# When ScalarE evacuates the down products: behind tanh, ahead of the fp16 conversion and the down weights

## What is computed

```
x  = L0_attn_x                              # 4 x 256 x 512
xn = _layernorm(x)
# attention: q 32 heads, k and v 8 heads, width 16, causal
weights = softmax(where(causal, -inf, q @ k.T) * 16 ** -0.5)
attn    = (weights @ v) @ Wo + bo
# experts: sigmoid scores, top 4 of 16, weights normalised
g, u = xn @ Wg[e].T, xn @ Wu[e].T           # 512 -> 256
out += cw[:, e] * ((silu(g) * u) @ Wd[e].T) # 256 -> 512
out += (silu(xn @ Sg.T) * (xn @ Su.T)) @ Sd.T
x + attn + out
```

## Time and profile before

| what | value |
|---|---|
| median of 3 runs | 598.5 us (597.1 to 607.98) |
| profiled execution, its own time | 602.74 us |
| its span, first to last instruction | 601.0 us |
| mean granted TensorE clock | 0.929 |
| TensorE matmuls busy | 474.4 us (79%) |
| VectorE busy | 372.9 us (62%) |
| ScalarE busy | 260.0 us (43%), 385 instructions |
| GpSimd busy | 251.3 us (42%) |

### The profile page before, as it was taken

The page is one execution under the profiler, slowest core; times in us unless marked ns, Lnnn a source line. Parts: engine busy times, 40 slices in busy tenths (PEclk is TensorE's granted clock), DMA queues, the critical chain, the costliest instruction groups (busy, mean ns, idle before and its releaser), DMA issues.

```text
span 601.0 us, 10314 instructions
## 1 busy us (share of the span) xinstructions
PE 474.4 (79%) x2984; PEld 349.3 (58%) x2984; DVE 372.9 (62%) x656; ACT 260.0 (43%) x385; POOL 251.3 (42%) x224
## 2 busy tenths in 40 slices
PE   0993679689976987889859788898688889889970
PEld 0872557456754764567636464676456647667640
DVE  6189866766863685448838881668556715966420
ACT  0531111255544473445547642556555425645610
POOL 3000491046544552264436672354445534545420
PEclk9996889879998997979979989999989989989986
DMA  7713924166355457655396945555853463425322
GB/s 288 290 54 93 306 65 126 70 207 175 68 156 132 74 142 201 122 141 98 66 247 189 270 100 107 109 147 116 247 148 62 82 116 65 80 54 82 45 36 35
DMA packets 33502, 78.26 MB, mean 130 GB/s; under 512 B 4960, under 2 KB 12640, under 8 KB 30240
## 3 DMA queue, kind: packets, MB, share of 16 engines
q0 software_dynamic: 11936, 27.53, 25.3%
q1 hardware_dynamic: 14064, 41.60, 20.9%
q10 hardware_dynamic: 7440, 8.39, 6.1%
HBM read 54.04 MB, written 23.33 MB: 129 GB/s over the span
## 4 chain that ended last, share of the span: by engine, by line
PE 47%; DVE 18%; issue 11%; ACTq 8%; ACT 6%; DMA 5%; POOL 2%; DVEq 1%; SPq 0%; POOLq 0%
PE psum L1051 26%; PE psum L1178 5%; DMA k_pack<-k_parts 4%; DVE negm L871 3%; PE psum L1012 2%; PE psum L1188 2%; ACT wsplit L517 2%; PE psum L1075 2%; PE psum L1144 2%; PE psum L1160 2%; ACTq L627 2%; ACTq L253 1%; ACTq L539 1%; PE psum L1061 1%; DMA xn<-x 1%
## 5 line engine op out<-in xcount | busy, mean ns | idle before, releaser
L1051 PE MATMUL psum<-wsplit,xgT 128*128 (+1 forms) x660 | 178.3, 421 | 9.2 <-DVE xgT L756 9.2
L1051 PEld LDWEIGHTS psum<-wsplit,xgT 128*128 128x128 f32 x660 | 128.2, 201 | 37.7 <-issue 9.8
L422 POOL DMA_INDIRECT out<-ysb,tab x48 | 83.3, 1736 | 128.2 <-ACT ysb L550 118.7
L1051 PE MATMUL psum<-wsplit,zT 128*128 (+1 forms) x336 | 98.9, 433 | 19.6 <-DVE zT L863 19.6
L1051 PEld LDWEIGHTS psum<-wsplit,zT 128*128 128x128 f32 x336 | 64.9, 204 | 38.4 <-issue 25.5
L591 ACT ACTIVATE xn<-psum 128x1536 f32<-128x1536 f32 x32 | 46.4, 1451 | 53.0 <-PE psum L1146 33.8
L402 POOL DMA_INDIRECT xg<-xn_rows,tab x47 | 51.2, 1089 | 39.5 <-PE psum L1188 22.1
L871 DVE TENSOR_REDUCE negm<-psum 128x4 f32<-128x512 f32 x64 | 58.4, 950 | 9.4 <-PE psum L1080 9.3
L911 DVE TENSOR_TENSOR xgT<-psum,xgT 128x512 fp32r<-128x512 f32 x47 | 32.3, 688 | 51.0 <-ACT xgT L513 45.9
L504 ACT ACTIVATE th<-psum 128x256 f32<-128x256 f32 x55 | 21.2, 386 | 95.5 <-PE psum L1051 92.7
L427 POOL TENSOR_TENSOR wsplit<-wraw,wsplit (+1 forms) x16 | 39.6, 2476 | 51.4 <-ACT wsplit L517 47.2
(11 more groups left out here) (174 smaller groups left out, 642.1 us busy)
## 6 DMA issues: line engine op xcount, KB each, us to landing
wraw<-wexp SPq DMA_DIRECT2D x17, 1024.0 KB
wraw<-wexp SPq DMA_DIRECT2D x17, 512.0 KB
q_parts<-stage ACTq DMA_DIRECT2D x36, 64.0 KB
q_pack<-q_parts ACTq DMA_DIRECT2D x6, 384.0 KB, 5.7
xn<-x SPq DMA_DIRECT2D x4, 512.0 KB, 5.7
xn_rows<-xn SPq DMA_DIRECT2D x8, 256.0 KB, 6.1
ctxs<-x SPq DMA_DIRECT2D x8, 256.0 KB, 3.8
out<-ysb SPq DMA_DIRECT2D x8, 256.0 KB, 3.0
```

Of the source, the lines that this page charges most:

```text
L422: nc.gpsimd.indirect_dma_start(out=out, out_offset=rows_of(s), in_=ysb[:, par, :], in_offset=None, compute_op=ALU.add).then_inc(y_out[par] ...
L1051: last = MM(dst, lhs(a, k), split_weights(place, w, c), start=m == 0, stop=m == len(products) - 1)
```

## The change

ScalarE's call of `y_evac(b, j)` moves from the end of the slot to right behind `tanh(s + U1, j % 2)`. It now stands in front of `high16`, of the three stores of the projected queries and of `down_high`. The other engines' lists are the same, row for row. One line moves, so the lines behind it up to the old place have a number that is higher by one.

```diff
@@ -618,6 +618,7 @@
                             minus_maxima(2 * b + (g // 4 + 1), 1 - g // 4)
                         if not (last and j == SPS - 1):
                             tanh(s + U1, j % 2)
+                        y_evac(b, j)
                         if j == BESIDE[g][0]:
                             high16(b, g)
                         if j == BESIDE[g][0] and g < QF and not last:
@@ -627,7 +628,6 @@
                                 act.dma_start(q_rows(b + 1, g, c), parts[:, c, g, :]).then_inc(parts_out[g], 16)
                         if not (last and j == SPS - 1):
                             down_high(s)
-                        y_evac(b, j)
```

## The result

The change made the kernel slower: 636.0 us (median of 4 runs, 633.28 to 640.25) against 600.63 us of the kernel before in the same comparison, a ratio of 1.062 with a 95% interval of 1.051 to 1.072. The forecast was +3.0% and 617 us, with 626 as its upper end. The direction was right, and the size is about twice what I gave. The profiled execution took 634.33 us (span 632.5, mean granted clock 0.922), which is 31.6 us more than the profiled one before (the spans differ by 31.5).

What follows compares the result with a forecast made beforehand. No engine was taken to own the span (TensorE 47%, ScalarE's sequencer 8%). The terms 5.7+7.4+1.0+1.2+2.9 = 18.2 us on the profiled 602.74 us gave a ratio of 1.030 and 617 us, range 603 to 626.

Steps and rivals of the forecast that it cites:

- steps 1 to 3: Groups with stores: evacuation starts when down ends, stores and numerators follow 3.8 us later, loop grows to 10.4 us; 5.7 us.
- rival (a): ScalarE's sequencer goes on past a waiting y_evac, so stores start where they do now; +2.1, 600 us; chance 0.08.
- term A: Six down-to-down loops in groups with stores get longer; 5.7 us, between 2 and 9.
- the sign: Groups with stores: tanh to tanh at 10.2 us or more in the profile after.
- step 4: Last group with stores before the k_pack loads, three times: x_high comes 4.94 us after down instead of 2.49.
- Term B: Late x_high before the k_pack loads, 3 x 2.45 = 7.4 us, low 3.9, high 8.5.
- step 5: Batch starts: z_transpose earlier but x_high later, three together +1.0 us, between -3 and +3; last batch without stores +1.2 us.
- step 6: Other 19 first slots without stores: high16 ends 2.2 us after down; 0.15 each, 2.9 us, between 0 and 8.
- (b): Delay in groups with stores and before k_pack loads half covered, 2 and 3.9 us; +9, 607.5 us; chance 0.17.
- (c): z_transpose is the bottleneck at batch starts and the last batch's end; all 6.4 us come back, 592 us; chance 0.03.

Runs made afterwards that it cites:

- e3: Against the kernel before: down_high directly behind high16, then y_evac, so only the stores stand behind the evacuation; 600.86 us, ratio 1.001.
- e7: The change, with the three stores of group 3 issued behind the k_pack loads of group 4; 626.99 us, ratio 1.046 to the kernel before.
- e9: The change, with only down_high's first register load in front of y_evac; branch, second load and conversion stay behind; 620.38 us, ratio 1.034 to the kernel before.
- e1: Against the kernel before: y_evac moved behind high16 and the three stores, in front of down_high only; 608.04 us, ratio 1.012.
- e2: Against the kernel before: y_evac moved behind high16, in front of the stores and down_high; 632.22 us, ratio 1.050.
- e4: The change's order in the 36 slots without stores, the order of the kernel before in the 12 with stores; 615.68 us, ratio 1.025 to that kernel.
- e10: The change, with down_high in front of y_evac in the 12 slots with stores only; 618.18 us, ratio 1.031 to the kernel before.
- e5: The change, with down_high in front of y_evac in all slots, then high16 and stores; 607.04 us, ratio 1.014 to the kernel before.
- e6: Against the kernel before: down_high moved directly behind tanh, ahead of high16 and the stores, y_evac still last; 590.96 us, ratio 0.986.
- e8: Against the kernel before: order high16, down_high, y_evac, stores, with group 3's stores behind the k_pack loads; 594.28 us, ratio 0.995.
- e11: Against the kernel before: down_high directly behind tanh, y_evac last, group 3's stores behind the k_pack loads; 592.37 us, ratio 0.987.
- e12: Against the kernel before: order down_high, high16, y_evac, stores, with group 3's stores behind the k_pack loads; 593.37 us, ratio 0.991.

## Why the prediction was right in direction and too small

**Right: steps 1 to 3.** That the stores are held back behind a waiting evacuation was inferred from the wait of `high16` in the earlier trace rows (it waited with stores behind it twice, until 272.19 and 405.84, and the first store followed 0.01 us later both times). The changed kernel shows it for the evacuation. In all 12 slots with stores ScalarE stood still in `y_evac` until the down products ended, and the first store began 0.09 to 0.10 us behind the evacuation's start (163.02 and 163.11 in the rows above), nowhere ahead of it. That refutes rival (a). `high16` did not hold them back where it only waited for the engine: it stands ahead of the stores and started at 163.60, half a microsecond after the first of them. The forecast loop was 10.4 us and the one shown took 10.69 (10.56 from tanh to tanh), the numerators were forecast at 3.8 us behind down and came at 4.0. The six loops of term A cost 7.0 us instead of 5.7. That agreement is in part luck: from tanh to tanh they took 9.27 to 14.33 us, three of them less than the 10.2 that I had named as the sign, and 4.4 of the 7.0 us lie in the two loops of the third batch, the only batch that converts down weights there; I had 1.9 for the conversion's loop. The four loops of the first two batches cost 2.6. What I hadn't seen is that it is a threshold, although both numbers stood in the text: 9.2 us for TensorE's loop and 6.6 behind the numerators leave 2.6, and e3 shows that the stores fit in there.

**Right in mechanism, small in size: step 4.** Term B was 7.4 us and the stretch lost 10.3. `x_high` came 5.5 us behind the evacuation's start and not 4.9, because the register load directly behind the stores took 1.15 us and then that of `slot_parts` 0.64. Moving the stores of group 3 away (e7) took 9 us off, inside the 9 to 12 forecast for it.

**The steps that failed: step 5, the batch starts (+1.0, measured +10.0), and step 6, the other slots (+1.8 in slots 7 to 11, measured +9.5).** Together that is 16.7 us that the forecast lacks, and A and B lack 4.2 more.

Step 5 let `x_high` be late by its path and found that TensorE's gate and up products cover nearly all of it. The third batch's start shows that alone, since neither of its slots has a conversion of down weights. `x_high` came 5.56 us behind the evacuation's start (404.81 against 399.25) and not 4.9. From `x_high` to the down products I took 2.0 us, though the rows that I named for it give 2.4 (500.60 to 502.97); here it was 1.9 (404.81 to 406.70). TensorE, no longer held up by `z_transpose`, was through with its gate and up products at 403.36 and stood idle until `z_low`:

```profile
406.70 2.25 PE L1051 MATMUL psum<-wsplit,zT 128*128 x6 [3.35 <-DVE zT L863]
```

and behind that idle time it ran at a lower granted clock (the third number from the right; columns as in the last section):

```profile
406.70:409.00 2.30, 2.30 (x7) 1.47 (x8) 2.09 (x2) 1.15 (x3) 0.00 (x0) 0.68 0.00 0
409.00:412.40 3.40, 3.40 (x13) 2.45 (x12) 1.02 (x3) 2.13 (x2) 2.15 (x2) 0.71 0.62 186
```

From 396.7 to 403.4 it had been 1.00, and the kernel before had 1.00 in the same work. The forecast had no term for the clock, and this start lost 3.1 us instead of 0.8. With the register load hoisted (e9) the idle time is 2.77 us, the granted clock stays at 1.00, and this start loses 0.9:

```profile
396.41 1.66 PE L1054 MATMUL psum<-wsplit,zT 128*128 x6 [2.77 <-DVE zT L866]
```

All three starts together lose 3.2 us in e9, where the conversions are still late, against 10.0. So the larger part of step 5's miss is the register load behind the stores and what follows from it.

Step 6, and step 5 at the second batch, priced the late conversion of the down weights too low. Term A gave it 1.9 us at one expert change. In steps 5 and 6 I followed `high16` into `low16` and called the rest covered ("its cover is gone where ScalarE also converts weights", 0.15 us each). But GpSimd waits for 15 conversions, and each is followed by GpSimd's `down_low` of 2.3 us or more before the down products of the next slot may start. With the change it starts behind the end of the previous down products at the earliest. The second batch's start in the changed kernel, ScalarE:

```profile
260.61 0.69 ACT L550 ACTIVATE ysb<-psum,tab 128x512 f32<-128x512 f32 x1 [2.91 <-PE psum L1051]
260.70 1.13 ACTq L628 DMA_DIRECT2D q_parts<-stage  x1
...
265.74 1.06 ACT L517 ACTIVATE wsplit<-wraw  x1 [3.07 <-issue]
```

Then GpSimd and TensorE:

```profile
267.12 2.35 POOL L427 TENSOR_TENSOR wsplit<-wraw,wsplit  x1 [10.33 <-ACT wsplit L517]
```

```profile
262.16 3.06 PE L1051 MATMUL psum<-wsplit,xgT 128*128 x12
...
269.61 2.92 PE L1051 MATMUL psum<-wsplit,zT 128*128 x6 [4.39 <-POOL wsplit L427]
```

The evacuation ends at 261.30, the stores and loads end 4.4 us later, conversion and low part follow, and the down products start at 269.61, with TensorE idle for 4.4 us ahead of them. I had forecast -0.6 us for this batch's start. It was +4.3, which I measured from tanh of slot 0 to tanh of slot 2 (22.09 against 17.76). Then six matmuls take 2.92 us instead of 1.66, with a granted clock of 0.50 in that stretch (269.6 to 272.5), behind the idle time. Here the register load counts as well: e9 leaves this conversion late and this start loses 0.1.

Slots 7 to 11 have no stores, and there the conversion shows by itself. In each of the seven orders that leave `down_high` behind the evacuation in these slots (the change, e1, e2, e4, e7, e9, e10) they lost 7.2 to 9.5 us, and in the six that put it in front (e3, e5, e6, e8, e11, e12) 0.1 to 3.9. e9 is among the seven with 7.2, so it isn't the first register load. GpSimd's wait goes the same way, 82 to 95 us in the seven and 43 to 47 in the six. By differences of ratios the cost is 1.8 points in the slots without stores (e10 to e5), and 2.0 points in all slots with the load already hoisted (e9 to e5).

**Wrong in the other sense: the end of a batch.** I had 0 there and it won 6.6 us, 6.1 in the first batch. It isn't the evacuation that won it; the last section has the rows.

**The rivals.** (b) and (c) fell with the time. (b) took A at 2 and B at 3.9; the stretches lost 7.0 and 10.3. (c)'s mechanism, the wait of L1061, did come back as 5.9 us (6.4 to 0.5) and was lost behind `x_high` and `down_high`. The best order that was tried is the opposite of the change: leave the evacuation last and move the short `down_high` forward (e6).

**Accounting.** 1.062 is made of: the register load behind the stores 2.8 points (change to e9), branch, second load and conversion behind the evacuation 2.0 (e9 to e5), `high16` and the rest 1.4 (e5 to before). These are differences of ratios, each uncertain by about one point.

## What to carry to other kernels

Moving an instruction that waits ahead in a list moved everything behind it into the shadow of that wait: the first of the stores began 0.09 to 0.10 us behind the evacuation's start in all 12 slots. Count the register loads and branches too (1.15 us for one load behind the stores), follow each conversion to the engine that consumes it, and read the granted clock behind idle time that is new on TensorE (0.68 behind 3.35 us, 0.50 behind 4.39 us). The delay on this path was free up to the other engine's loop time less what lies behind the delay, 9.2-6.6 = 2.6 us: at 2.44 us (e3) the loop stayed at 9.19, at 3.96 it was 1.4 to 1.5 us longer. So work out such a threshold before you sum. If bookkeeping sits between two engines' handovers, try moving that forward and leave the wait last: here it gave -1.4% (-1.9 to -0.8) where the change gave +6.2%.

## What the runs showed of the hardware

A register load on ScalarE's sequencer took 0.28 us in the median (123 of them in either kernel). Directly behind three DMA starts that of `down_high` took 0.80 to 1.07 us before and 0.81 to 1.24 with the change (12 each). Three starts take 2.3 us, the first of them 1.1.

The output projection (16 matmuls, L1178) ran at different speeds in the two kernels. Before the change, TensorE in the first batch:

```profile
233.47 1.97 PE L1170 MATMUL psum<-ident,ctxs 128*128 128x128 f32 x8 [2.91 <-DVE ctxs L949]
235.45 9.22 PE L1178 MATMUL psum<-wo_sb,stage 128*128 128x512 f32 x16
```

With the change:

```profile
241.42 1.09 PE L1170 MATMUL psum<-ident,ctxs 128*128 128x128 f32 x8 [1.23 <-DVE ctxs L949]
242.94 7.11 PE L1178 MATMUL psum<-wo_sb,stage 128*128 128x512 f32 x16 [0.42 <-ACT stage L602]
```

The windows by stage show the clock. Columns are the stretch, its length, each engine's busy time, the granted clock, the DMA share and GB/s. Before:

```profile
233.00:235.40 2.40, 1.93 (x8) 1.57 (x8) 0.41 (x1) 0.60 (x1) 1.86 (x2) 0.50 0.55 232
235.40:244.70 9.30, 9.26 (x17) 3.76 (x16) 0.69 (x1) 0.60 (x1) 0.00 (x0) 0.77 0.97 189
```

With the change:

```profile
242.90:250.00 7.10, 7.06 (x16) 2.96 (x16) 0.69 (x1) 0.38 (x1) 3.62 (x2) 1.00 0.99 248
```

After 2.91 us of idle time the granted clock was 0.50 in the transposes and still 0.77 over the projection; after 1.23 us it was 1.00 over the projection. Transposes and projection together took 11.2 us before and 8.6 with the change, 2.6 us of the 6.1 won at that batch's end. In the other three batches of both kernels the projection took 7.1 us, behind 1.1 to 2.0 us of idle time. In the first batch of e9 it took 8.8 us behind 1.5 us of idle time, so the idle time directly ahead is not all that decides it.

Why the idle time was longer before is in VectorE's and GpSimd's rows. Before:

```profile
230.93 2.34 POOL L427 TENSOR_TENSOR wsplit<-wraw,wsplit  x1 [5.35 <-ACT wsplit L517]
```

```profile
231.75 1.67 DVE L949 TENSOR_TENSOR ctxs<-csum,den 128x128 f32<-128x128 f32 x1
```

With the change:

```profile
242.58 2.35 POOL L427 TENSOR_TENSOR wsplit<-wraw,wsplit  x1 [7.68 <-ACT wsplit L517]
```

```profile
241.07 0.29 DVE L949 TENSOR_TENSOR ctxs<-csum,den 128x128 f32<-128x128 f32 x1
```

The last operation of `context` took 1.67 us while GpSimd's `down_low` ran beside it, and ended 0.15 us after `down_low` did. With the change `down_low` comes later and the same operation took 0.29. It is so in the runs too: 1.50 to 1.66 us where `down_low` ran beside it (e3, e5, e6, e8, e11, e12), 0.29 where it came later (e1, e2, e4, e7, e9, e10). So at this one place the late conversion won something: 1.4 us of VectorE's time, and in this pair of kernels the 2.6 us at the higher clock behind it. The other 2 us of the 6.1 stay open.
